# Second attention of a two-layer block: one run of scores and one run of outputs for each sequence, in place of two halves apart

## The chip, the core and the metric

The kernel runs on one core of one Trainium2 chip. The metric is the device time of one execution in microseconds (us); lower is better.

## The reference, cut to what matters

Sixteen sequences of 128 tokens of width 128 go through two blocks: cross attention and a mixture of experts, and then a second cross attention and a second mixture of experts. The change lies in the second attention. It has 16 heads of width 64 and reads the keys and values of a context of 128 tokens, the last 4 of which have weights of their own and a softmax of their own:

```python
def _attention(q_in, k_in, v_in):
    q = _split_heads(q_in); k = _split_heads(k_in); v = _split_heads(v_in)
    s = jnp.einsum('bhid,bhjd->bhij', q, k) * SCALE
    p = jax.nn.softmax(s, axis=-1)
    return _merge_heads(jnp.einsum('bhij,bhjd->bhid', p, v))
...
q_in = x @ Wq + _lora(x, q_down, q_up, q_alpha)
k_in = org_ctx @ Wk + _lora(org_ctx, k_down, k_up, k_alpha)
v_in = org_ctx @ Wv + _lora(org_ctx, v_down, v_up, v_alpha)
out = _attention(q_in, k_in, v_in)
out_ipa = _attention(q_in, ipa_ctx @ Wk_ipa, ipa_ctx @ Wv_ipa)
out = out + IPA_SCALE * out_ipa
return out @ Wo + bo + _lora(out, o_down, o_up, o_alpha)
```

## The kernel before

Each of the five engines runs a program of its own, in the order in which its code is written; nothing is scheduled by a planner. The engines meet only through semaphores: an instruction adds to one when it is done, and `wait_ge` holds an engine, with all that is queued behind it, until a count is there.

**The rounds.** Each engine walks through `body(b)` for b from -2 to 16. A round b works on three sequences: it takes the scores and the softmax of sequence b, prepares queries, keys and values of the next one, f = b + 1, and finishes the one before, t = b - 1 (the softmax weights are turned, multiplied by the values and projected). Rounds 1 to 14 have all three; round 0 has no t, and round 15 no f.

**The pieces on TensorE** (`@block.tensor`). `scores(b, half)` at line 1194 takes eight heads; a head is only 64 deep, so two heads lie on the upper and lower 64 rows of the array and follow each other as pairs. `turn(t, n)` (L1205, n from 0 to 3) transposes the weights of four heads. `queries(f, n)` (L1214), `keys(f, n)` (L1222) and `values(f, n)` (L1241) are projections in two halves each. `outputs(t, n)` (L1234) takes eight heads; a head's result is 64 wide, so two heads lie on the left and right 64 columns of the array. L1274 turns the normalized input of sequence b + 2, and L1282 is the output projection. Scores have the array cut in rows, outputs have it cut in columns, and all other pieces use it whole.

**PSUM.** Eight banks are shared out by hand. Scores use banks 0 to 3. Queries, turned weights and outputs go through banks 4 and 5, keys and turned weights through bank 6, values through banks 5 and 6, and the projection through bank 7. Each piece waits (`freed, count`) until the former content of its bank was copied out. Both halves of the keys go to bank 6, so `keys(f, 1)` waits on `Z.k0_sb` for the copy of the first half.

**VectorE** (`@block.vector`). `shifted(b, n)` (L664, L665, L667) takes the maxima of four heads and subtracts one from the four extra scores; ScalarE's exponentials wait for it. `turned(t, n)` (L673) copies turned weights out of PSUM. `summed(b, n)` (L679, L681) makes the sums and their reciprocals. L713 copies the first half of the keys to `k1T` and signals `Z.k0_sb`. L306, L310 and L301 are the residual, its statistics and the next normalized input.

**ScalarE** (`@block.scalar`). `powers(b, n)` (L923) takes four exponentials; `queries` (L930), `outputs` (L935) and `values` (L940) copy those results out of PSUM; L956 is the exponential of the extra scores, L961 the copy of the second half of the keys (`Z.k1_sb`), L967 the copy of the turned input.

**GpSimd** multiplies the weights by the reciprocals (L473), and SyncE loads the values of the four extra tokens by one DMA for each sequence. Neither is touched.

Of the kernel before, what the change touches and what calls it, by code (L numbers as in the profile page):

```python
# [26 lines left out]
CH = 4  # L27
# [15 lines left out]
def there(b):  # L43
    return not isinstance(b, int) or 0 <= b < B
# [19 lines left out]
def build_program(nc, T, out):  # L64

    with ExitStack() as ctx:
# [35 lines left out]
        class Arena:  # L102
# [9 lines left out]
            def take(self, shape, dt=F32):  # L112
# [8 lines left out]
                if dt != F32:  # L121
# [151 lines left out]
        Z = named(sem, "z", "xn xb tr xT q q_sb k0 k1 k0_sb k1_sb ki v v_sb vi0 vi1 score ipa_max maxed ipa_exp ipa_step ipa_p "  # L273
                            "exp sum rsum norm turned p_sb o o_sb proj x_new stats")
# [225 lines left out]
        def _(dve):  # L500
# [158 lines left out]
            def shifted(b, n):  # L659

                got_s = blocks(bank[n])
                part = slice(CH * n, CH * n + CH)
                dve.wait_ge(Z.score, CH * b + n + 1)
                dve.tensor_reduce(ipa_max[:, b % 2, part], got_s[:, :, ORG:S], X, ALU.max).then_inc(Z.ipa_max, 1)  # L664
                dve.tensor_reduce(negmax1[:, b % 2, part], got_s[:, :, 0:ORG], X, ALU.max, negate=True)  # L665
                dve.wait_ge(Z.ipa_max, CH * b + n + 1)
                dve.tensor_tensor(ipa_s[:, b % 2, part, :], got_s[:, :, ORG:S],  # L667
                                  ipa_max[:, b % 2, part].unsqueeze(2).broadcast_to((128, CH, IPA)), ALU.subtract).then_inc(Z.maxed, 1)
# [25 lines left out]
            def body(b):  # L694
                f, t = b + 1, b - 1
                if there(b):
                    shifted(b, 0)
                if there(t):
                    turned(t, 0)
                if there(b):  # L700
                    shifted(b, 1)
                if there(t):
                    turned(t, 1)
                if there(b):
                    summed(b, 0)
                    shifted(b, 2)
                if there(t):
                    turned(t, 2)
                if there(b):
                    shifted(b, 3)  # L710
                if there(f):
                    dve.wait_ge(Z.k0, f + 1)
                    dve.tensor_copy(k1T[:, f % 2, 0:4, 0:ORG], bank[6][:, 0:4 * ORG].rearrange("p (c n) -> p c n", c=4))\  # L713
                        .then_inc(Z.k0_sb, 1)
                if there(t):
                    turned(t, 3)
                if there(b):
                    summed(b, 1)
                    summed(b, 2)
                if there(b):  # L720
                    summed(b, 3)
                    ipa_norm(b)
                if there(t):
                    dve.wait_ge(Z.proj, t + 1)
                    dve.wait_ge(Z.xb, t + 1)
                    dve_residual(dve, Z, t, bank[7][:, 0:D])
                    dve_stats(dve, Z, t)
                if there(b + 3):
                    xn1_of(b + 3)
# [103 lines left out]
            with dve.Fori(0, B // 2) as i:  # L833
                for u in range(2):
                    b = i * 2 + u
# [4 lines left out]
        def _(act):  # L840
# [91 lines left out]
            def outputs(t, n):  # L932

                act.wait_ge(Z.o, 2 * t + n + 1)
                act.activation(o1T[:, 4 * n:4 * n + 4, :], blocks(bank[5 - n]), ACT.Copy).then_inc(Z.o_sb, 1)  # L935
# [6 lines left out]
            def body(b):  # L942
                f, t = b + 1, b - 1
                if there(b):
                    powers(b, 0)
                if there(f):
                    queries(f, 0)
                if there(b):
                    powers(b, 1)
                if there(f):  # L950
                    queries(f, 1)
                if there(b):
                    powers(b, 2)
                if there(b):
                    powers(b, 3)
                    act.activation(ipa_s[:, b % 2, :, :], ipa_s[:, b % 2, :, :], ACT.Exp).then_inc(Z.ipa_exp, 1)  # L956
                if there(t):
                    outputs(t, 0)
                if there(f):
                    act.wait_ge(Z.k1, f + 1)  # L960
                    act.activation(k1T[:, f % 2, 4:8, 0:ORG], bank[6][:, 0:4 * ORG].rearrange("p (c n) -> p c n", c=4), ACT.Copy)\  # L961
                        .then_inc(Z.k1_sb, 1)
                if there(t):
                    outputs(t, 1)
                if there(b + 2):
                    act.wait_ge(Z.tr, b + 3)
                    act.activation(xT[:, b % 2, :], bank[7][:, 0:128], ACT.Copy).then_inc(Z.xT, 1)  # L967
                if there(f):
                    values(f, 0)
                    values(f, 1)  # L970
# [53 lines left out]
        def _(pe):  # L1024
# [19 lines left out]
            def scores(b):  # L1044

                pe.wait_ge(A.negT_sb, b + 1)
                pe.wait_ge(A.qm, b + 1)
                pe.wait_ge(A.cT, 4)
                after(pe, A.exp, 2 * b)
                for g in range(CH):  # L1050
                    for i in range(4):
                        pe.matmul(SC0[:, i, 128 * g:128 * g + 128], pick0[tile_rows(i), g, :], negmax0T[tile_rows(i), b % 2, :],
                                  start=(g == 0), stop=False)
                for i in range(4):
                    mm = pe.matmul(SC0[:, i, :], k0T[tile_rows(i), b % 4, :], qm0[tile_rows(i), b % 4, :, :],  # L1055
                                   start=False, stop=True)
                    if i % 2 == 1:
                        mm.then_inc(A.score, 1)
# [166 lines left out]
            def outputs(t, n, freed, count):  # L1225

                pe.wait_ge(Z.p_sb, CH * t + 2 * n + 2)
                pe.wait_ge(Z.v_sb, 2 * t + n + 1)
                pe.wait_ge((Z.vi0, Z.vi1)[t % 2], 16 * (t // 2 + 1))
                after(pe, freed, count)  # L1230
                for c in range(CH):
                    for odd in range(2):
                        h = 8 * n + 2 * c + odd
                        mm = pe.matmul(blocks(bank[5 - n])[D1 * odd:D1 * odd + D1, c, :], v1[:, t % 2, D1 * h:D1 * h + D1],  # L1234
                                       p1T[:, CH * (2 * n + odd) + c, :], start=True, stop=True)
                mm.then_inc(Z.o, 1)
# [7 lines left out]
            def body(b):  # L1244
                f, t = b + 1, b - 1
                if there(b):
                    scores(b, 0)
                if there(t):
                    turn(t, 0, Z.o_sb, 2 * t)
                if there(f):  # L1250
                    queries(f, 0, Z.v_sb, 2 * f - 1)
                if there(t):
                    turn(t, 1, Z.v_sb, 2 * min(f, B))
                if there(f):
                    queries(f, 1, *((Z.p_sb, CH * t + 1) if there(t) else (Z.q_sb, 2 * f)))
                if there(b):
                    scores(b, 1)
                if there(t):
                    turn(t, 2, *((Z.q_sb, 2 * f + 1) if there(f) else (Z.v_sb, 2 * B - 1)))
                if there(f):  # L1260
                    keys(f, 0, *((Z.p_sb, CH * t + 2) if there(t) else (Z.v_sb, 2 * f)))
                if there(t):
                    turn(t, 3, *((Z.q_sb, 2 * f + 2) if there(f) else (Z.p_sb, CH * t + 1)))
                    outputs(t, 0, Z.p_sb, CH * t + 3)
                if there(f):
                    keys(f, 1, Z.k0_sb, f + 1)
                if there(t):
                    outputs(t, 1, Z.p_sb, CH * t + 4)
                if there(f):
                    values(f, 0, *((Z.o_sb, 2 * t + 1) if there(t) else (Z.q_sb, 2 * f + 1)))  # L1270
                if there(b + 2):
                    pe.wait_ge(Z.xn, b + 3)
                    after(pe, Z.x_new, b - 1)
                    pe.transpose(bank[7][:, 0:128], xn[:, b % 2, :], ident[:, :]).then_inc(Z.tr, 1)  # L1274
                if there(f):
                    values(f, 1, Z.k1_sb, f + 1)
                if there(t):
                    pe.wait_ge(Z.o_sb, 2 * t + 2)
                    after(pe, Z.xT, min(b + 3, B))
                    after(pe, Z.x_new, t)  # L1280
                    for c in range(8):
                        mm = pe.matmul(bank[7][:, 0:D], o1T[:, c, :], wo1[:, c, :], start=(c == 0), stop=(c == 7))  # L1282
                    mm.then_inc(Z.proj, 1)
# [101 lines left out]
```

## Time and profile before

| | |
|---|---|
| median of 3 runs | 611.37 us (610.2 to 611.38) |
| the profiled execution | 611.36 us, its span 609.7 us |
| TensorE busy | 517.7 us, 85% of the span |
| VectorE busy | 419.5 us, 69% |
| ScalarE busy | 288.1 us, 47% |
| GpSimd busy | 136.2 us, 22% |
| the second attention, first scores to last projection | 226.4 to 452.1 us |

The profile is of one execution. What a change within one stage is worth is read from that stage, by its timeline on each engine, not from the shares of the whole span. In the profile, a matmul in f32 has two records, so a group of eight matmuls is shown as x16. Starts of matmuls are recorded, while their ends are modelled and overlap the next group; a piece's cost is therefore read from its start to the start of the next piece.

### The profile page before, as it was taken

How to read it: one execution, taken by the hardware profiler on the slowest of the kernel's cores; microseconds unless marked ns; L12 is line 12 of the kernel's file. 1: busy time of each engine (PE TensorE's matmuls, PEld its weight loads, DVE VectorE, ACT ScalarE, POOL GpSimd, SP SyncE). 2: the span in 40 equal slices, each digit the busy share in tenths (PEclk: the TensorE clock that was granted, in tenths of full speed). 3: DMA queues.
4: the chain of work that ended last, by engine and by line, in shares of the span. 5: the costliest groups of instructions: out<-in, count | busy, mean ns of one | idle time of the engine just before them, and what ended most of it. 6: DMA issues, size and time to landing. Idle time of an engine off the chain costs nothing. (4 is left out here: it accounts for less than half of the span.)

```text
span 609.7 us, 13056 instructions
## 1 busy us (share of the span) xinstructions
PE 517.7 (85%) x4669; PEld 378.7 (62%) x4669; DVE 419.5 (69%) x1140; ACT 288.1 (47%) x728; POOL 136.2 (22%) x197
## 2 busy tenths in 40 slices
PE   1698888648999369999999999999856689999977
PEld 1455555437443157888888888888645335666667
DVE  3588888553769939777677777777653745777762
ACT  1354545212345227666555666666414473555530
POOL 3644433010000113333322233233420110000000
PEclk9989999975899979999999999999888799999989
DMA  7900000000000030000000000000000000222102
GB/s 177 212 3 3 2 2 3 2 1 1 0 1 1 1 110 1 4 2 3 2 3 4 2 3 2 3 3 3 2 0 1 1 0 27 79 77 77 53 4 66
DMA packets 21990, 14.35 MB, mean 24 GB/s; under 512 B 6056, under 2 KB 21264, under 8 KB 21936
## 3 DMA queue, kind: packets, MB, share of 16 engines
q1 hardware_dynamic: 21936, 13.61, 8.5%
q8 instruction: 36, 0.59, 0.4%
q14 instruction: 18, 0.15, 0.1%
HBM read 12.30 MB, written 1.05 MB: 22 GB/s over the span
## 5 line engine op out<-in xcount | busy, mean ns | idle before, releaser
L923 ACT ACTIVATE early<-bank,negmax 128x124 f32<-128x124 f32 x256 | 72.6, 375 | 62.0 <-DVE ipa_s L667 62.0
L473 POOL TENSOR_TENSOR early<-early,rsum 128x496 f32<-128x496 f32 x64 | 63.9, 1020 | 151.3 <-DVE rsum L681 151.3
L1342 PE MATMUL bank<-late,early 128*128 (+1 forms) x128 | 59.2, 608 | 2.0 <-ACTq L296 2.0
L863 ACT ACTIVATE early<-bank 128x1024 f32<-128x1024 f32 x32 | 31.0, 1022 | 30.6 <-PE bank L1055 30.6
L673 DVE COPY wide<-bank 128x512 f32<-128x512 f32 x64 | 43.2, 679 | 0.0
L665 DVE TENSOR_REDUCE negmax<-bank 128x4 f32<-128x496 f32 x64 | 42.4, 663 | 0.0
L548 DVE TENSOR_REDUCE negmax<-bank 128x8 bf16<-128x1024 f32 x32 | 39.0, 1220 | 4.2 <-PE bank L1040 3.8
L679 DVE TENSOR_REDUCE sums<-early 128x4 f32<-128x496 f32 x64 | 41.4, 647 | 0.5 <-ACT early L923 0.5
L815 DVE TENSOR_TENSOR late<-late,bank 128x512 f32<-128x512 f32 x32 | 22.0, 687 | 28.6 <-ACT late L1010 27.4
L1342 PEld LDWEIGHTS bank<-late,early 128*128 128x128 f32 x128 | 23.7, 195 | 27.4 <-issue 24.1
L1205 PE MATMUL bank<-ident,early 128*128 128x128 f32 x256 | 39.7, 280 | 1.1 <-DVE wide L673 1.1
L412 POOL TENSOR_TENSOR rstd<-veps,minus_half 128x14 f32<-128x14 f32 (+3 forms) x8 | 13.2, 1649 | 121.5 <-DVE veps L507 121.5
L306 DVE TENSOR_TENSOR x_all<-bank,x_all 128x128 f32<-128x128 f32 x32 | 9.2, 286 | 44.6 <-PE bank L1282 43.4
L1234 PE MATMUL bank<-wide,late 128*64 128x128 f32 x512 | 35.7, 283 | 2.7 <-DVE wide L673 2.7
L1282 PEld LDWEIGHTS bank<-late,wide 128*128 128x128 f32 x256 | 32.5, 200 | 8.8 <-issue 5.1
L1222 PE MATMUL bank<-cT_all,late 96*128 96x124 f32 x256 | 35.7, 283 | 1.9 <-DVE late L713 1.9
L1194 PE MATMUL bank<-late 64*128 64x128 f32 x512 | 37.2, 285 | 0.0
L1214 PE MATMUL bank<-xT,late 128*128 128x128 f32 x256 | 35.4, 285 | 0.4 <-ACT xT L967 0.4
L1354 PEld LDWEIGHTS bank<-early,late 128*128 128x128 f32 x256 | 30.9, 192 | 7.2 <-issue 7.2
L1178 PE MATMUL bank<-early 128*128 128x512 f32 x64 | 30.8, 609 | 4.9 <-DVE early L628 4.2
L1222 PEld LDWEIGHTS bank<-cT_all,late 96*128 96x128 f32 x256 | 31.4, 193 | 4.8 <-DVE late L713 4.7
L1194 PEld LDWEIGHTS bank<-late 64*128 64x128 f32 x512 | 31.1, 187 | 5.2 <-issue 1.7
(193 smaller groups left out, 1085.0 us busy)
## 6 DMA issues: line engine op xcount, KB each, us to landing
early<-in_L_ffn_w_dram SPq DMA_DIRECT2D x48, 128.0 KB, 2.2
out_dram<-x_all SPq DMA_DIRECT2D x16, 64.0 KB, 1.6
x_all<-in_x_dram SPq DMA_DIRECT2D x1, 768.0 KB, 6.9
ctx_all<-in_ctx_dram SPq DMA_DIRECT2D x1, 576.0 KB, 8.6
early<-in_L_ffn_We_dram SPq DMA_DIRECT2D x1, 512.0 KB
late<-in_L_xattn_Wq_dram SPq DMA_DIRECT2D x1, 512.0 KB, 6.8
late<-in_L_xattn_Wo_dram SPq DMA_DIRECT2D x1, 512.0 KB, 8.4
late<-in_L_xattn_Wk_dram SPq DMA_DIRECT2D x1, 384.0 KB, 6.6
```

The costliest lines, as they stand in the source:

```text
L473: pool.tensor_tensor(part, part, rsum1[:, b % 2, CH * n:CH * n + CH].unsqueeze(2).broadcast_to((128, CH, ORG)), ALU.mult).then_inc(Z.norm, 1)
L548: dve.tensor_reduce(to, MAX0.rearrange("p i (g n) -> p i g n", g=CH), X, ALU.max, negate=True)\
L665: dve.tensor_reduce(negmax1[:, b % 2, part], got_s[:, :, 0:ORG], X, ALU.max, negate=True)
L673: dve.tensor_copy(p1T[:, CH * n:CH * n + CH, :], blocks(bank[(4, 6, 5, 4)[n]])).then_inc(Z.p_sb, 1)
L679: dve.tensor_reduce(sums1[:, b % 2, part], p1[:, b % 2, n, :, 0:ORG], X, ALU.add).then_inc(Z.sum, 1)
L923: ins = act.activation(p1[:, b % 2, n, c, 0:ORG], blocks(bank[n])[:, c, 0:ORG], ACT.Exp, bias=negmax1[:, b % 2, CH * n + c:CH * n + c + 1])
L1194: mm = pe.matmul(blocks(bank[2 * half + odd])[:, c, :], q1T[rows, b % 2, CH * half + c, :], k1T[rows, b % 2, CH * half + c, :], start=True ...
L1205: mm = pe.transpose(blocks(bank[(4, 6, 5, 4)[n]])[:, c, :], p1[:, t % 2, n, c, :], ident[:, :])
L1214: mm = pe.matmul(blocks(bank[5 - n])[:, c, :], wq1[:, part], xT[:, f % 2, :], start=True, stop=True)
L1222: mm = pe.matmul(bank[6][:, ORG * c:ORG * c + ORG], wk1[0:C, part], cT_all[:, f, 0:ORG], start=True, stop=True)
L1234: mm = pe.matmul(blocks(bank[5 - n])[D1 * odd:D1 * odd + D1, c, :], v1[:, t % 2, D1 * h:D1 * h + D1], p1T[:, CH * (2 * n + odd) + c, :], s ...
L1342: mm = pe.matmul(bank[2 * c + n][:, :], w[:, q % 4, 128 * c:128 * c + 128], xgT[:, :, e, :], start=True, stop=True)
```

## The change

The same instructions with the same operands run on each engine; only their order is another. On TensorE, `scores(b, 1)` follows `scores(b, 0)` at once, and `outputs(t, 0)` stands behind `keys(f, 1)`, right before `outputs(t, 1)`. On VectorE, the copy of the first half of the keys stands ahead of `shifted(b, 3)`. On ScalarE, `outputs(t, 0)` stands behind the copy of the second half of the keys.

```diff
@@ VectorE, body(b)
                 if there(t):
                     turned(t, 2)
-                if there(b):
-                    shifted(b, 3)
                 if there(f):
                     dve.wait_ge(Z.k0, f + 1)
                     dve.tensor_copy(k1T[:, f % 2, 0:4, 0:ORG], bank[6][:, 0:4 * ORG].rearrange("p (c n) -> p c n", c=4))\
                         .then_inc(Z.k0_sb, 1)
+                if there(b):
+                    shifted(b, 3)
                 if there(t):
                     turned(t, 3)
@@ ScalarE, body(b)
-                if there(t):
-                    outputs(t, 0)
                 if there(f):
                     act.wait_ge(Z.k1, f + 1)
                     act.activation(k1T[:, f % 2, 4:8, 0:ORG], bank[6][:, 0:4 * ORG].rearrange("p (c n) -> p c n", c=4), ACT.Copy)\
                         .then_inc(Z.k1_sb, 1)
                 if there(t):
+                    outputs(t, 0)
                     outputs(t, 1)
@@ TensorE, body(b)
                 if there(b):
                     scores(b, 0)
+                    scores(b, 1)
                 if there(t):
                     turn(t, 0, Z.o_sb, 2 * t)
...
                 if there(f):
                     queries(f, 1, *((Z.p_sb, CH * t + 1) if there(t) else (Z.q_sb, 2 * f)))
-                if there(b):
-                    scores(b, 1)
                 if there(t):
                     turn(t, 2, *((Z.q_sb, 2 * f + 1) if there(f) else (Z.v_sb, 2 * B - 1)))
                 if there(f):
                     keys(f, 0, *((Z.p_sb, CH * t + 2) if there(t) else (Z.v_sb, 2 * f)))
                 if there(t):
                     turn(t, 3, *((Z.q_sb, 2 * f + 2) if there(f) else (Z.p_sb, CH * t + 1)))
-                    outputs(t, 0, Z.p_sb, CH * t + 3)
                 if there(f):
                     keys(f, 1, Z.k0_sb, f + 1)
                 if there(t):
+                    outputs(t, 0, Z.p_sb, CH * t + 3)
                     outputs(t, 1, Z.p_sb, CH * t + 4)
```

TensorE in round 1, before, from the first scores (L1194) over turn (L1205), queries (L1214), keys (L1222) and outputs (L1234) to the second outputs:

```order
L1194 MATMUL bank<-late 128x128 x8
L1205 MATMUL bank<-ident,early 128x128 x4
L1214 MATMUL bank<-xT,late 128x128 x4
L1205 MATMUL bank<-ident,early 128x128 x4
L1214 MATMUL bank<-xT,late 128x128 x4
L1194 MATMUL bank<-late 128x128 x8
L1205 MATMUL bank<-ident,early 128x128 x4
L1222 MATMUL bank<-cT_all,late 128x124 x4
L1205 MATMUL bank<-ident,early 128x128 x4
L1234 MATMUL bank<-wide,late 64x128 x8
L1222 MATMUL bank<-cT_all,late 128x124 x4
L1234 MATMUL bank<-wide,late 64x128 x8
```

The same stretch of the changed kernel, where the line numbers of these pieces are lower by one:

```order
L1193 MATMUL bank<-late 128x128 x16
L1204 MATMUL bank<-ident,early 128x128 x4
L1213 MATMUL bank<-xT,late 128x128 x4
L1204 MATMUL bank<-ident,early 128x128 x4
L1213 MATMUL bank<-xT,late 128x128 x4
L1204 MATMUL bank<-ident,early 128x128 x4
L1221 MATMUL bank<-cT_all,late 128x124 x4
L1204 MATMUL bank<-ident,early 128x128 x4
L1221 MATMUL bank<-cT_all,late 128x124 x4
L1233 MATMUL bank<-wide,late 64x128 x16
```

Four pieces on a cut array have become two of twice the length, and between the two halves of the keys there is now one turn, in place of a turn and an outputs piece.

VectorE in round 1, before, from `shifted(b, 2)` on: L664, L665 and L667 are one `shifted`, L673 is a `turned`, L713 the copy of the first half of the keys:

```order
L664 TENSOR_REDUCE ipa_max<-bank 128x4
L665 TENSOR_REDUCE negmax<-bank 128x4
L667 TENSOR_TENSOR ipa_s<-bank,ipa_max 128x16
L673 COPY wide<-bank 128x512
L664 TENSOR_REDUCE ipa_max<-bank 128x4
L665 TENSOR_REDUCE negmax<-bank 128x4
L667 TENSOR_TENSOR ipa_s<-bank,ipa_max 128x16
L713 COPY late<-bank 128x4x124
L673 COPY wide<-bank 128x512
```

The same stretch of the changed kernel, where that copy is line 711:

```order
L664 TENSOR_REDUCE ipa_max<-bank 128x4
L665 TENSOR_REDUCE negmax<-bank 128x4
L667 TENSOR_TENSOR ipa_s<-bank,ipa_max 128x16
L673 COPY wide<-bank 128x512
L711 COPY late<-bank 128x4x124
L664 TENSOR_REDUCE ipa_max<-bank 128x4
L665 TENSOR_REDUCE negmax<-bank 128x4
L667 TENSOR_TENSOR ipa_s<-bank,ipa_max 128x16
L673 COPY wide<-bank 128x512
```

The copy has moved ahead of one `shifted`, three instructions.

## Rows read from the trace of the kernel before

**Rows 1.** Windows (stretch, length, busy time of engines, PEclk): rounds; end of stage.

```profile
222.00:437.00 215.00, 211.11 (x2013) 177.17 (x2012) 162.12 (x478) 133.06 (x392) 68.78 (x89) 1.00 0.02 6
437.00:443.90 6.90, 6.02 (x35) 5.65 (x36) 3.08 (x11) 1.84 (x6) 4.69 (x7) 0.51 0.01 2
```

**Rows 2.** Timeline of TensorE, round 6: start us, us, instruction, [idle before <- releaser].

```profile
305.07 1.16 PE L1194 MATMUL bank<-late 64*128 64x128 f32 x16
306.16 0.66 PE L1205 MATMUL bank<-ident,early 128*128 128x128 f32 x4
306.65 1.06 PE L1214 MATMUL bank<-xT,late 128*128 128x128 f32 x8
307.55 0.60 PE L1205 MATMUL bank<-ident,early 128*128 128x128 f32 x4
307.98 1.06 PE L1214 MATMUL bank<-xT,late 128*128 128x128 f32 x8
308.97 1.16 PE L1194 MATMUL bank<-late 64*128 64x128 f32 x16
310.06 0.66 PE L1205 MATMUL bank<-ident,early 128*128 128x128 f32 x4
...
311.45 0.60 PE L1205 MATMUL bank<-ident,early 128*128 128x128 f32 x4
311.98 1.09 PE L1234 MATMUL bank<-wide,late 128*64 128x128 f32 x16
313.00 1.16 PE L1222 MATMUL bank<-cT_all,late 96*128 96x124 f32 x8
314.09 1.09 PE L1234 MATMUL bank<-wide,late 128*64 128x128 f32 x16
315.11 1.12 PE L1241 MATMUL bank<-late,cT_all 96*124 96x512 f32 x2
...
318.92 1.16 PE L1194 MATMUL bank<-late 64*128 64x128 f32 x16
```

**Rows 3.** Timeline of TensorE at the first and last rounds.

```profile
232.88 1.16 PE L1222 MATMUL bank<-cT_all,late 96*128 96x124 f32 x8 [1.16 <-DVE late L713]
...
437.19 1.97 PE L1234 MATMUL bank<-wide,late 128*64 128x128 f32 x16 [0.25 <-DVE wide L673]
...
447.37 1.97 PE L1234 MATMUL bank<-wide,late 128*64 128x128 f32 x32 [0.57 <-DVE wide L673]
```

**Rows 4.** Timeline of VectorE, round 6.

```profile
306.26 0.17 DVE L664 TENSOR_REDUCE ipa_max<-bank 128x4 f32<-128x16 f32 x1 [0.22 <-PE bank L1194]
...
307.01 0.68 DVE L673 COPY wide<-bank 128x512 f32<-128x512 f32 x1
307.61 0.16 DVE L664 TENSOR_REDUCE ipa_max<-bank 128x4 f32<-128x16 f32 x1
...
312.26 0.66 DVE L713 COPY late<-bank 128x496 f32<-128x496 f32 x1
312.84 0.68 DVE L673 COPY wide<-bank 128x512 f32<-128x512 f32 x1
313.44 0.66 DVE L679 TENSOR_REDUCE sums<-early 128x4 f32<-128x496 f32 x1
...
314.22 0.64 DVE L679 TENSOR_REDUCE sums<-early 128x4 f32<-128x496 f32 x1
```

**Rows 5.** Timeline of ScalarE, round 6.

```profile
307.13 1.13 ACT L923 ACTIVATE early<-bank,negmax 128x124 f32<-128x124 f32 x4 [3.14 <-DVE ipa_s L667]
308.13 0.61 ACT L930 ACTIVATE late<-bank 128x512 f32<-128x512 f32 x1
308.61 1.16 ACT L923 ACTIVATE early<-bank,negmax 128x124 f32<-128x124 f32 x4
...
313.38 0.27 ACT L956 ACTIVATE ipa_s<-ipa_s 128x64 f32<-128x64 f32 x1
313.52 0.61 ACT L935 ACTIVATE wide<-bank 128x512 f32<-128x512 f32 x1
```

## The prediction

> **What bounds the kernel now.** I first read the windows of the profile over the second attention. From 222 to 437 us TensorE is busy 211.1 of 215.0 us, at a granted clock of 1.00, while VectorE has 162.1 us and ScalarE 133.1 us [rows 1]. So I next read TensorE's timeline for one round. From the scores at 305.07 to those at 318.92 us no row has an idle time: the round lasts 13.85 us and is pure TensorE time [rows 2]. Rounds 1 to 14 repeat it (scores start at 235.80 us in round 1 and every 13.85 us after). A shorter TensorE order therefore shortens the kernel, but only until another engine is late. For that I then read the timelines of VectorE and ScalarE for the same round [rows 4, 5]. All times below with no other zero are counted from the round's first scores, so 305.07 is 0.
>
> **TensorE: what is saved.** The reader should compare how long the same piece takes by its neighbours [rows 2].
> - Queries take 0.90 (306.65 to 307.55) before a turn, but 0.99 (307.98 to 308.97) before scores.
> - A turn takes 0.43 between whole-array pieces (307.55 to 307.98), 0.49 behind scores (306.16 to 306.65), and 0.53 before outputs (311.45 to 311.98).
> - Scores take 1.09. Turn 2 and the first keys together take 1.39 (310.06 to 311.45), so these keys take 0.90, as queries do.
> - Outputs take 1.02 each, and the second keys, between two of them, take 1.09.
>
> Each border between a cut and a whole array thus costs about 0.1 on the piece outside, and some more lies inside the cut piece. In the last round two outputs pieces follow each other: 1.97 for x32, against 1.09 for x16 alone [rows 3, 2], so a second outputs piece adds 0.88 and not 1.02. For scores no row shows two pieces in a row. The bounds are 1.09 (nothing saved inside) and 0.90 (eight pairs at the pace of the eight records of queries); I take 0.90, since outputs behave so.
>
> The new round on TensorE, if nothing waits: scores 1.09 + 0.90 = 1.99; turn 0.49; queries 0.90; turn 0.43; queries 0.90; turn 0.43; keys 0.90; turn 0.43; keys before outputs 0.99; outputs 1.02 + 0.88 = 1.90; and from the first values to the next scores 3.81, unchanged (315.11 to 318.92). The sum is 13.17, which is 0.68 less than 13.85. Over 14 rounds that would be 9.5 us.
>
> **The cover that goes.** The second keys need bank 6, and so wait for VectorE's copy of the first keys. Before, this copy ran from 312.26 to 312.92, and the keys began at 313.00 [rows 4, 2]: it landed just in time, 0.08 ahead. The change takes 1.0 us of outputs away from before these keys, and 1.1 us of scores too. In return it moves the copy ahead of one `shifted`. I walk VectorE's chain up to the copy.
> - The first `shifted` starts at 1.19, as before; it waits for the first half of the scores only [rows 4]. It takes 0.75 (306.26 to 307.01), to 1.94.
> - Then comes the first `turned`. Before, its turn was long done. Now the turn starts at 1.99, behind all scores, and ends at 2.65 (0.66 after its start [rows 2]). With the 0.03 that VectorE takes to follow (scores end at 305.07 + 1.16 = 306.23, and it starts at 306.26) this `turned` starts at 2.68: a **new wait of 0.74** at the head of the chain.
> - From there it runs through: `turned` 0.60 (307.01 to 307.61), `shifted` 0.75, `turned` 0.60, `summed` 0.78 (313.44 to 314.22), `shifted` 0.75, `turned` 0.60. That is 4.08, so the copy starts at 6.76 and ends at 7.42. What these steps wait for is earlier: the second turn starts at 3.38 and ends at 3.98, before 4.03; the scores of banks 2 and 3 are ready at 2.0.
> - The second keys start 0.08 later, at 7.50.
>
> TensorE reaches them at 1.99 + 0.49 + 0.90 + 0.43 + 0.90 + 0.43 + 0.90 + 0.43 = 6.47. So it stands **idle for 1.03 us** there in each round. Bounds: were all of VectorE's steps as short as their issue allows and turn 0 followed at once, the copy could come 0.1 earlier; if the two scores pieces take 2.18 instead of 1.99, turn 0 and all of the chain come 0.19 later. Queued behind the waiting keys is all of TensorE's round: both outputs, values, projection and the next scores.
>
> **After the stall.** Keys 0.99, to 8.49; outputs 1.90, to 10.39, where the first values start if bank 5 is free. For that ScalarE must have copied the first outputs. The fourth `shifted` now starts behind the copy, at 6.76 + 0.58 (312.26 to 312.84) = 7.34. Exponentials start 0.87 after their `shifted` (306.26 to 307.13), at 8.21, and take 1.00 (307.13 to 308.13); the extra exponential 0.14 (313.38 to 313.52), to 9.35; the copy of the second keys 0.48 (as 308.13 to 308.61), to 9.83; the copy of the outputs ends 0.61 later, at 10.44 [rows 5]. TensorE follows some 0.05 behind, since the 0.08 above is an upper end: the values start at 10.49, another 0.10 late. Then 3.81: the round ends at **14.30**. Bounds for this second wait are 0 and 0.13.
>
> So a round goes from 13.85 to 14.30, up 0.45: 0.68 saved, 1.03 + 0.10 lost. The second outputs need the fourth `turned`, which ends at 7.34 + 0.75 + 0.68 = 8.77, before 9.4. VectorE's remaining sums end near 11.8 and its residual waits for the projection as before. GpSimd's multiplications follow these sums, and what needs them is the second to fourth turn of the next round, from 14.30 + 3.38 on. These cost nothing, with more than a microsecond of cover. SyncE's small DMA of the extra values waits for the second outputs of a round and is needed a round later. It has some ten microseconds of cover.
>
> **The edges.** Round 0 has no turn. There the second keys already wait 1.16 us for the copy [rows 3], and the copy moves ahead by one `shifted`, 0.75, and by the wait for later scores; but ScalarE's own copy of the second keys, behind all exponentials, is next late. I take -0.2, between 0 and -1.0. In round 15 there are no keys; all outputs wait for VectorE's chain (the second at 437.19 has such a wait [rows 3]), which gets the new 0.74 of turn 0 and loses nothing: +0.7.
>
> **Sum.** 14 x 0.45 = 6.3, - 0.2 + 0.7 = +6.8. The span of the profiled run, 609.7 us, becomes 616.5, and with the 1.66 outside it (611.36 - 609.7), 618.2. The median of the runs, 611.37, is the same as this execution. With the cheap ends of the bounds (stall 0.9, no second wait, round 0 at -1.0) a round is 14.07 and the time 614; with the dear ends for the waits 14.35 and 619.
>
> **Two rules beside the rows.** The Trainium skill, on the page TensorEngine Tiling (Array Packing), section Key Properties, says that a change of tiling mode drains TensorE. By that rule alone the result is the 9.5 us gain above, since four such borders go in each round; rows 2 bear it out in size. The same page, section PSUM Bottleneck, says that a faster TensorE can leave the copies out of PSUM as the limit. By it the result is 14.30 a round; VectorE's copy at 312.26 with 0.08 to spare is where the trace agrees.
>
> **Rivals.**
> - *The cover holds, and the saving arrives* (faster). This needs the copy to start by about 5.8 instead of 6.76, that is, the wait at turn 0 must not be there or VectorE must catch it up. For it: VectorE is only 75% busy in the stage [rows 1]. Against: its free time lies behind its sums, while the chain from first scores to the copy has no slack left. A round of 13.17 gives -9.5 - 0.2 + 0.7: 602.4 us. Chance 0.08.
> - *Saving and stall cancel.* With a stall of only 0.6 to 0.75 the round is within 0.1 of 13.85, and the time within 1.2 us (0.2%, about what a measurement here can tell) of 611.4. Nothing in the rows makes the chain 0.4 shorter. Chance 0.06.
> - *Borders don't cost what I think* (the change doesn't do what it says): each group of eight carries its own cost. Then scores take 2.18 and outputs 2.04, turn 0 and so the keys come 0.19 later, and the round is 7.69 + 0.99 + 2.04 + 3.81 = 14.53: 14 x 0.68 + 0.9 gives 621.8. The x32 row of 1.97 speaks against [rows 3]. Chance 0.06.
> - *The clock falls.* With over 1 us idle in a round the granted clock could fall as it did at 437 us, where outputs took 1.97 for x16 instead of 1.09 and the stretch 437.0 to 443.9 has 0.51 [rows 3, 1]. A stretch like that costs about half of its 6.0 us of TensorE time, 3 us. Against: a wait of 1.16 us in round 0 left it at 1.00 [rows 3, 1]. Two such stretches give 624. Chance 0.06.
>
> **How the numbers follow.** The forecast has 0.70 (618.2), and 0.04 is left for dearer things I don't see. Slower: 0.70 + 0.06 + 0.06 + 0.04 = 0.86; same 0.06; faster 0.08. The range takes in the forecast with its bounds and the two dear rivals: 613.5 to 624. It leaves out the faster case, the cancelling one and the dearest.
>
> **What would show it.** Right: TensorE's timeline has 1.0 us idle before the second keys in each round, released by VectorE's copy; VectorE has 0.7 idle before its first `turned`, released by the turn; the scores' x32 takes about 2.0 and the outputs' 1.9; the first values have about 0.1 idle, released by ScalarE; rounds are 14.2 to 14.4 apart. Wrong: no idle before the second keys, or a first `turned` that starts at 1.9; scores that take 2.2; or a clock below 1.00 between rounds 1 and 14.

## The result and the profile after

| | before | changed |
|---|---|---|
| median | 611.37 us (6 runs, 605.15 to 611.75) | 617.14 us (6 runs, 614.01 to 618.85) |
| the profiled execution | 611.36 us, span 609.7 | 618.85 us, span 617.2 |
| TensorE busy | 517.7 us | 513.8 us |
| a round of the second attention (1 to 14) | 13.85 us | 14.27 us |

The ratio is 1.0107, 95% interval 1.0061 to 1.0154: the kernel became slower by 1.1%, although TensorE is busy 3.9 us less. (The medians alone lie 5.8 us apart, 0.9%.)

TensorE's timeline of round 5 of the changed kernel answers to [rows 2]. Its lines are lower by one, the projection's by two: 1193 are scores, 1204 turns, 1213 queries, 1221 keys, 1233 outputs, 1240 values, 1280 the projection.

```profile
294.06 2.06 PE L1193 MATMUL bank<-late 64*128 64x128 f32 x32
296.05 0.66 PE L1204 MATMUL bank<-ident,early 128*128 128x128 f32 x4
296.54 1.06 PE L1213 MATMUL bank<-xT,late 128*128 128x128 f32 x8
297.44 0.60 PE L1204 MATMUL bank<-ident,early 128*128 128x128 f32 x4
297.87 1.06 PE L1213 MATMUL bank<-xT,late 128*128 128x128 f32 x8
298.77 0.60 PE L1204 MATMUL bank<-ident,early 128*128 128x128 f32 x4
299.20 1.05 PE L1221 MATMUL bank<-cT_all,late 96*128 96x124 f32 x8
300.09 0.60 PE L1204 MATMUL bank<-ident,early 128*128 128x128 f32 x4
301.51 1.16 PE L1221 MATMUL bank<-cT_all,late 96*128 96x124 f32 x8 [0.82 <-DVE late L711]
302.60 1.97 PE L1233 MATMUL bank<-wide,late 128*64 128x128 f32 x32
304.52 1.12 PE L1240 MATMUL bank<-late,cT_all 96*124 96x512 f32 x2
...
308.33 2.06 PE L1193 MATMUL bank<-late 64*128 64x128 f32 x32
```

From scores to scores it is 14.27 us. The scores of 16 heads take 1.99 (294.06 to 296.05), and the outputs 1.92. Up to the last turn TensorE is ahead by what the scores' borders gave. Then comes the only idle time of the round: the second keys start 1.42 behind the turn (300.09 to 301.51), where a turn takes 0.43. That is 0.99 us lost; the row shows 0.82, since the modelled end of the turn overlaps it.

VectorE, same round, answers to [rows 4]. L711 is the copy of the first keys:

```profile
295.25 0.17 DVE L664 TENSOR_REDUCE ipa_max<-bank 128x4 f32<-128x16 f32 x1 [0.22 <-PE bank L1193]
...
296.74 0.69 DVE L673 COPY wide<-bank 128x512 f32<-128x512 f32 x1 [0.65 <-PE bank L1204]
...
298.69 0.66 DVE L679 TENSOR_REDUCE sums<-early 128x4 f32<-128x496 f32 x1
...
300.80 0.66 DVE L711 COPY late<-bank 128x496 f32<-128x496 f32 x1
301.38 0.16 DVE L664 TENSOR_REDUCE ipa_max<-bank 128x4 f32<-128x16 f32 x1
```

The first `turned` (L673) starts 2.68 after the scores, released by the turn on TensorE. Without that wait it would have started at 1.94, as in [rows 4]. From there nothing waits until the copy, which starts at 6.74 and ends at 7.40; the keys follow at 7.45.

ScalarE, same round: L935 are the copies of both outputs. The first of the two ends near 304.46 (0.61 after its start, as such a copy takes in [rows 5]), the first values start at 304.52:

```profile
303.38 0.60 ACT L959 ACTIVATE late<-bank 128x496 f32<-128x496 f32 x1
303.85 1.37 ACT L935 ACTIVATE wide<-bank 128x512 f32<-128x512 f32 x2
```

The list of waits from 227 to 440 us, rounds 0 to 14 and the first turns of round 15, shows how often. Its columns are total us, times, longest:

```profile
PE bank L1221 <- DVE late L711: 12.2, 15, 0.8
DVE wide L673 <- PE bank L1204: 9.8, 15, 0.7
PEld bank L1240 <- ACT wide L935: 2.7, 14, 0.2
```

### The profile page after: what moved, and what is told of

Its sections match the earlier page's. It is cut to its first block and busy times, and to the rows that moved or that the text cites. A ratio compares the mean times of both kernels' runs of the same rounds, so it can differ in the third digit from the quotient of the medians.

```text
span 617.2 us, 13056 instructions
## 1 busy us (share of the span) xinstructions
PE 513.8 (83%) x4669; PEld 377.7 (61%) x4669; DVE 419.5 (68%) x1140; ACT 288.9 (47%) x728; POOL 136.1 (22%) x197
## 5 line engine op out<-in xcount | busy, mean ns | idle before, releaser
L673 DVE COPY wide<-bank 128x512 f32<-128x512 f32 x64 | 43.4, 681 | 9.8 <-PE bank L1204 9.8
L665 DVE TENSOR_REDUCE negmax<-bank 128x4 f32<-128x496 f32 x64 | 42.4, 663 | 0.0
L548 DVE TENSOR_REDUCE negmax<-bank 128x8 bf16<-128x1024 f32 x32 | 39.1, 1221 | 3.3 <-PE bank L1039 2.9
L1177 PE MATMUL bank<-early 128*128 128x512 f32 x64 | 32.6, 639 | 4.9 <-DVE early L628 4.2
L1233 PE MATMUL bank<-wide,late 128*64 128x128 f32 x512 | 32.6, 280 | 3.6 <-DVE wide L673 3.6
L1280 PE MATMUL bank<-late,wide 128*128 128x128 f32 x256 | 33.1, 285 | 1.4 <-ACT wide L935 1.4
L1240 PE MATMUL bank<-late,cT_all 96*124 96x512 f32 x64 | 33.4, 616 | 0.4 <-ACT late L959 0.4
```

Source lines behind the costliest of these rows:

```text
L548: dve.tensor_reduce(to, MAX0.rearrange("p i (g n) -> p i g n", g=CH), X, ALU.max, negate=True)\
L673: dve.tensor_copy(p1T[:, CH * n:CH * n + CH, :], blocks(bank[(4, 6, 5, 4)[n]])).then_inc(Z.p_sb, 1)
```

## The experiments

Each ratio below is to the kernel before, run beside the experiment (its median was 610.49 us beside the first four and 611.47 beside the last three). The length of a round is the better measure, since only the order within it was changed.

Two kinds of theory were to be told apart. Mine: each switch between a cut and a whole array costs TensorE some 0.17 us (the forecast's 0.68 over four), the change saves four of them a round, and it loses more because the copy of the first keys no longer lands in time. The rivals: the run of scores itself, or VectorE's whole chain, sets the pace whatever stands behind; or the saving is not in the switches.

### Scores together, outputs apart

The changed kernel, with the outputs and ScalarE's copies back in the old order (the cut shows TensorE only). VectorE's order stays as changed.

```diff
                 if there(t):
                     turn(t, 3, ...)
+                    outputs(t, 0, Z.p_sb, CH * t + 3)
                 if there(f):
                     keys(f, 1, Z.k0_sb, f + 1)
                 if there(t):
-                    outputs(t, 0, Z.p_sb, CH * t + 3)
                     outputs(t, 1, Z.p_sb, CH * t + 4)
```

> Only the scores follow one another; the outputs stand apart as before, and VectorE's copy of the first keys stays ahead of the fourth shifted, as in the changed kernel. My theory (the second keys wait for VectorE's copy because 1.0 us of outputs no longer stands before them): the copy still ends 7.4 us into the round, but the second keys now come 1.0 us later, so their wait goes. Instead the first outputs wait some 0.3 us for the third turned (bank 5). Round 13.8 us (13.85 before, 14.27 in the changed kernel), time 611.5. Rival (the run of scores itself is what costs, since VectorE's chain starts 0.7 us later and sets the round, whatever TensorE's order behind it is): round 14.2 or more, time 617.

Measured: 611.06 us, ratio 1.0017 (0.996 to 1.0074), so no difference. Rounds are 13.91 us. TensorE, in this kernel L1232 outputs, L1220 keys:

```profile
299.41 0.60 PE L1203 MATMUL bank<-ident,early 128*128 128x128 f32 x4
300.35 1.09 PE L1232 MATMUL bank<-wide,late 128*64 128x128 f32 x16 [0.33 <-DVE wide L673]
301.37 1.16 PE L1220 MATMUL bank<-cT_all,late 96*128 96x124 f32 x8
```

The wait is no longer before the keys but before the outputs in front of them, for the third `turned`, and it is 0.41 by starts (0.94 behind the turn, against 0.53 in [rows 2]). It eats what the borders of the scores gave. Those are 0.34 by [rows 2]: 0.19 in the second scores, 0.09 on the queries before them and 0.06 on the turn behind. So 13.85 - 0.34 + 0.41 = 13.92. The rival's 14.2 did not come, though VectorE had the same late start.

### Outputs together, scores apart

The changed kernel, with the second scores back where they stood before.

```diff
                 if there(b):
                     scores(b, 0)
-                    scores(b, 1)
...
                     queries(f, 1, ...)
+                if there(b):
+                    scores(b, 1)
```

> Only the outputs follow one another, with the copies on VectorE and ScalarE moved as in the changed kernel; the scores stand apart as before. My theory: VectorE has no wait at its first turned, but the second half of the scores now stands before turn 2, so the copy ends at 7.2 us, and the second keys would start at 6.8: they wait 0.5 us. Round 14.1 us, time 615.2. Rival (the run of scores is what costs): this change alone saves its borders, round 13.5 us, time 607.

Measured: 614.12 us, ratio 1.0081 (1.0028 to 1.0135); rounds 14.13 us. L1219 are the keys:

```profile
298.62 0.60 PE L1202 MATMUL bank<-ident,early 128*128 128x128 f32 x4
299.55 1.16 PE L1219 MATMUL bank<-cT_all,late 96*128 96x124 f32 x8 [0.33 <-DVE late L711]
300.63 1.97 PE L1231 MATMUL bank<-wide,late 128*64 128x128 f32 x32
```

Here VectorE does not start late, and the keys still wait, 0.50 by starts (0.93 against 0.43). So the loss does not need the run of scores: taking the outputs from between the two halves of the keys is enough for a loss of 0.28 us a round.

### The copy put back behind the fourth shifted

The changed kernel, with one VectorE piece moved.

```diff
                     turned(t, 2)
+                if there(b):
+                    shifted(b, 3)
                 if there(f):
                     dve.wait_ge(Z.k0, f + 1)
                     ...
-                if there(b):
-                    shifted(b, 3)
```

> The changed kernel with VectorE's copy of the first keys put back behind the fourth shifted. My theory: the copy is on the path that sets the round, so 0.75 us more before it shows: second keys 1.7 us idle by the natural order, round 14.9 to 15.0 us (14.27 in the changed kernel), time 626. Rival (VectorE's whole round or ScalarE sets the pace, not this copy): the order of two VectorE pieces doesn't matter, round 14.3, time 617.

Measured: 640.88 us, ratio 1.0507 (1.0438 to 1.0576). The direction is as my theory had it, but the size is double: some 30 us above the kernel before, where 626 would have been 15. Four of the 14 rounds take 14.99 us, as expected; ten take 16.62. TensorE in one of the long ones (L1219 keys, L1231 outputs), and two windows: the first over most of these outputs, the second over what follows, up to the next scores. After stretch, length and the busy time of the five rows of engines, their last columns are the granted clock, the DMA share and GB/s:

```profile
309.56 1.16 PE L1219 MATMUL bank<-cT_all,late 96*128 96x124 f32 x8 [1.57 <-DVE late L713]
310.65 3.01 PE L1231 MATMUL bank<-wide,late 128*64 128x128 f32 x32
313.58 1.71 PE L1238 MATMUL bank<-late,cT_all 96*124 96x512 f32 x2
```

```profile
311.40:314.80 3.40, 3.40 (x26) 2.55 (x21) 1.54 (x7) 1.19 (x2) 3.11 (x5) 0.50 0.00 0
314.80:318.00 3.20, 3.20 (x23) 2.29 (x21) 0.00 (x0) 1.36 (x3) 0.00 (x0) 1.00 0.03 5
```

The wait is 1.57 us instead of 0.82 in all 14 rounds. In ten of them the granted clock then falls from 1.00 to 0.50, that is from 2.4 to 1.2 GHz: the outputs take 2.93 by starts instead of 1.89, the values 1.55 instead of 0.96, and together 1.63 us more are lost. So the copy is on the path that sets the round, and with a wait that is 0.75 us longer the clock fell too, though not in every round: the four short ones have the same wait. In the changed kernel itself the clock stayed at 1.00 from round 1 to round 14.

### VectorE takes a shifted where it had to wait for the turn

The changed kernel, with VectorE's first pieces in another order.

```diff
                     shifted(b, 0)
+                    shifted(b, 1)
                 if there(t):
                     turned(t, 0)
                 if there(b):
-                    shifted(b, 1)
+                    summed(b, 0)
                 if there(t):
                     turned(t, 1)
                 if there(b):
-                    summed(b, 0)
                     shifted(b, 2)
```

> The changed kernel with VectorE's order shifted 0, shifted 1, turned 0, summed 0, turned 1: what it does at 1.94 us is then a shifted, whose scores are there, and not a turned that must wait for turn 0. My theory: the 0.74 us of new wait at the first turned is the cause of half of the stall; without it the copy ends 0.5 us earlier (it then waits 0.2 us for the keys themselves), the second keys wait 0.5 instead of 1.0 us, round 13.76 us, time 610. Rival (the order before the copy doesn't matter, or the wait at the turn only moves slack): round 14.27, time 617.

Measured: 609.29 us, ratio 0.9991 (0.9946 to 1.0037): no slower than before, with rounds of 13.78 us. L1219 are the keys:

```profile
295.44 1.05 PE L1219 MATMUL bank<-cT_all,late 96*128 96x124 f32 x8
296.33 0.60 PE L1202 MATMUL bank<-ident,early 128*128 128x128 f32 x4
297.25 1.16 PE L1219 MATMUL bank<-cT_all,late 96*128 96x124 f32 x8 [0.33 <-DVE late L711]
298.34 1.97 PE L1231 MATMUL bank<-wide,late 128*64 128x128 f32 x32
```

The wait at the turn was 0.5 of the 0.99 us, and its removal gives just that back (14.27 to 13.78). The rest is the missing cover, and no order on VectorE can win it. The list of waits from 250 to 430 us has the copy itself waiting for the first keys, in ten of its rounds:

```profile
DVE late L711 <- PE bank L1219: 1.5, 10, 0.2
```

VectorE is early now, and the copy can't start before its keys are done. From the start of the first keys to that of the second it is 1.81 us (295.44 to 297.25). With one turn between the two, TensorE has only 0.89 + 0.43 = 1.32 us of work for it, and 0.49 stay idle. The kernel before had 2.44 us between the two starts, from this row to 313.00 in [rows 2]:

```profile
310.56 1.05 PE L1222 MATMUL bank<-cT_all,late 96*128 96x124 f32 x8
```

### Both outputs ahead of the second keys

The change with cover put back. TensorE does both outputs before the second keys; ScalarE copies in the new order. VectorE's round begins with shifted 0, shifted 1, turned 0, turned 1, shifted 2, turned 2, shifted 3, turned 3; then come the copy of the first keys and all four summed.

```diff
@@ TensorE
                     turn(t, 3, ...)
-                if there(f):
-                    keys(f, 1, Z.k0_sb, f + 1)
-                if there(t):
                     outputs(t, 0, Z.p_sb, CH * t + 3)
                     outputs(t, 1, Z.p_sb, CH * t + 4)
                 if there(f):
+                    keys(f, 1, Z.k0_sb, f + 1)
                     values(f, 0, ...)
@@ ScalarE
+                if there(t):
+                    outputs(t, 0)
+                    outputs(t, 1)
                 if there(f):
                     act.wait_ge(Z.k1, f + 1)
                     ...
-                if there(t):
-                    outputs(t, 0)
-                    outputs(t, 1)
```

> The changed kernel with the second keys behind both outputs (TensorE: turn 3, outputs 0, outputs 1, keys 1; ScalarE copies in that order), VectorE in the order shifted 0, shifted 1, turned 0, turned 1, shifted 2, turned 2, shifted 3, turned 3, copy of the first keys, and then the four summed. Both runs stay together, and the 1.9 us of outputs cover the copy. My theory (the change failed only by the cover it took away): no wait on TensorE, the copy ends near 7.4 us and the second keys start at 8.4 us; round 13.17 us, time 601 to 602. Rival (whatever the order, VectorE or ScalarE can't deliver a round in much less than 13.8 us once the scores come in one run): round 13.7 or more, time 609 or more.

Measured: 600.21 us, ratio 0.9825 (0.9799 to 0.9851). It beats both kernels. The round is 13.26 us, without idle time on TensorE (L1189 scores, L1200 turns, L1229 outputs, L1217 keys, L1236 values):

```profile
300.38 2.06 PE L1189 MATMUL bank<-late 64*128 64x128 f32 x32
...
306.41 0.60 PE L1200 MATMUL bank<-ident,early 128*128 128x128 f32 x4
306.94 2.06 PE L1229 MATMUL bank<-wide,late 128*64 128x128 f32 x32
308.94 1.16 PE L1217 MATMUL bank<-cT_all,late 96*128 96x124 f32 x8
309.93 1.02 PE L1236 MATMUL bank<-late,cT_all 96*124 96x512 f32 x2
...
313.64 2.06 PE L1189 MATMUL bank<-late 64*128 64x128 f32 x32
```

VectorE's copy starts at 307.68 and would end at 308.35, 0.59 ahead of the keys. So the runs of scores and of outputs do pay, 0.59 us a round, once nothing waits. (TensorE's, VectorE's and ScalarE's order changed together here; which of the three it needs was not tried.) The rival, that VectorE or ScalarE can't deliver a round much below 13.8, falls. I had expected 13.17. The sum was 0.09 short, since I had used the changed kernel's: here the turn has outputs behind it and takes 0.53 instead of 0.43, the outputs take 2.00 (306.94 to 308.94) instead of 1.90, and from the first values to the next scores it is 3.71 instead of 3.81. The two runs do not pay alike. From the first scores to the first keys' end it is 6.03 instead of 6.38, so the scores' run gives 0.35. From there to the next scores it is 7.23 instead of 7.47, so the outputs' run gives 0.24.

### A turn between the two scores

```diff
                 if there(b):
                     scores(b, 0)
-                    scores(b, 1)
                 if there(t):
                     turn(t, 0, Z.o_sb, 2 * t)
+                if there(b):
+                    scores(b, 1)
                 if there(f):
                     queries(f, 0, Z.v_sb, 2 * f - 1)
```

(against the kernel of the last experiment)

> As keys_last, but turn 0 stands between the two scores pieces (scores 0, turn 0, scores 1, queries 0). The work is the same and nothing new waits, so the round shows what one more pair of borders between a cut and a whole array costs. My theory: 0.34 us more (0.10 on the turn's or queries' side, the rest inside the second scores): round 13.51 us, 14 to 16 x 0.34 = 5 us more than keys_last. Rival (what is saved lies in the halves' own start, or in banks, not in the switch): scores behind a turn cost no more than scores behind scores, round 13.2 us.

Measured: 606.81 us, ratio 0.9927 (0.9891 to 0.9962); rounds 13.65 us, 0.39 more, and again no idle time:

```profile
303.96 1.16 PE L1189 MATMUL bank<-late 64*128 64x128 f32 x16
305.06 0.66 PE L1200 MATMUL bank<-ident,early 128*128 128x128 f32 x4
305.64 1.16 PE L1189 MATMUL bank<-late 64*128 64x128 f32 x16
306.73 1.16 PE L1209 MATMUL bank<-xT,late 128*128 128x128 f32 x8
307.73 0.60 PE L1200 MATMUL bank<-ident,early 128*128 128x128 f32 x4
```

The two scores pieces take 1.10 + 1.09 instead of 1.99, the turn between them 0.58 instead of 0.49, and the queries behind scores 1.00 instead of 0.89. One more pair of borders is 0.39 us, where I had expected 0.34. It is the neighbour that costs, not the piece: the rival of a cost in the halves' own start falls.

### The changed kernel once more

> The changed kernel again, beside keys_last on the same chip. Theory: rounds of 14.27 us with 0.8 us idle shown before the second keys, time 617, some 15 us above keys_last. Rival: a few us of the difference to the kernel before come from stages ahead of the second attention; then its time moves with the start of the first scores, and the rounds stay at 14.27.

Measured: 616.94 us, ratio 1.0098 (1.0063 to 1.0133), rounds 14.28 us, first scores at 225.29 us where the first profile of it had 227.73. So the rounds repeat to 0.01 us, while the start of the stage moves by 2.4 us between executions of one kernel. In the stretch from 126 to 157 us TensorE's granted clock was 0.52 in the first profile and 0.67 in this one. The spans differ by less, 617.2 and 615.7 us, so what follows the rounds moves too. That such stages make the spread of the single times is likely, but only these two profiles show it. It is why the rounds tell more than the totals.

## Why the prediction was right, point by point

Forecast 618.2, measured 617.14, and slower with 0.86. The mechanism came as forecast; inside the sum two terms were off, and the total hides it.

**What TensorE saves: somewhat less.** Scores 1.99 as forecast, outputs 1.92 for 1.90. The value taken for two scores in a row, 0.90 added and not 1.09, had no row of before behind it; it came out as the outputs' pace had suggested. But the second keys take 1.09 (301.51 to 302.60) and not 0.99, which I had taken from pieces that follow a turn; behind a wait they are as long as [rows 2] showed them between two outputs. Without the idle time the round is 14.27 - 0.99 = 13.28, so 0.57 is saved and not 0.68: 0.35 by the scores, as the 0.34 of the rows, and 0.22 by the outputs. That each of the four borders gives 0.17 holds for the scores only.

**The cover that goes: right, to 0.05 us.** The first `turned` starts at 2.68 (forecast 2.68), the copy at 6.74 (6.76), the keys at 7.45 (7.50), lost 0.99 (1.03). The walk through VectorE's chain with durations of before was enough, since no duration changed.

**After the stall: the wait for ScalarE is there, but hardly shows.** The forecast had keys of 0.99, TensorE ready for the values at 10.39, and ScalarE's copy of the first outputs releasing them at 10.49. Measured, the longer keys bring TensorE there at about 10.43 (7.45 + 1.09 + 1.89, the outputs' length in a short round with the copy put back, 327.27 to 329.16). ScalarE's copy ends near 10.40 for the 10.44 forecast, and the values start at 10.46. The later of the two decides, so the keys' error cost nothing, and of the second wait of 0.10 some 0.03 is left. That this error of 0.10 fell where a wait had already been counted is luck. The 0.2 us on the weight load [the third line of the waits] is no measure of ScalarE's delay: with the copy put back, the same load has 0.17 idle where ScalarE had itself been waiting for the outputs. The round is 14.27 for 14.30: 0.57 saved and 0.99 lost, for the 0.68 and 1.13 of the forecast.

**The edges: right.** Round 0 went from 9.40 to 9.26 (-0.14, forecast -0.2): the keys' wait fell from 1.16 to 0.77, and the second values then waited 0.39 for ScalarE's copy of the second keys, which the prediction had named as next late. In round 15, from the scores to the second outputs, 7.56 became 8.30 (+0.74, forecast +0.7).

**The sum.** Rounds 1 to 14 give 199.66 - 193.83 = +5.83 us (forecast 6.3, whose 0.45 a round should have been 0.42). With the edges it is +6.43 of the 6.8. The profiled executions differ by 7.5 in span, of which 1.33 us lie before the first scores (226.40 and 227.73), in stages whose code is the same. The ratio of the runs, 1.0107, is 6.5 us, the medians differ by 5.8. A single total is thus right to a few us at best, and the hit to 1.1 us is in part luck; the 0.42 a round is what the prediction rests on.

**The rivals.** That the cover holds was false here, and true in the kernel with both outputs first. That borders cost nothing is refuted by the turn between two scores. That saving and stall cancel was not the change's case, but is that of its half with only the scores together, and of the reordered VectorE. That the clock falls did not happen at 0.99 us lost a round, and did with the copy put back, at 1.74, in ten rounds of 14.

**The two rules.** The Trainium skill, TensorEngine Tiling (Array Packing), section Key Properties, says that a change of tiling mode drains TensorE. No trace here shows a drain as such; they show a price, 0.39 us for one more pair of borders at the scores and 0.22 to 0.24 for the pair that the outputs' run saves. The section PSUM Bottleneck says that copies out of PSUM may become the bottleneck. In the changed kernel the copy of the first keys does set the round. But it was a matter of order, and not of how much is copied: with the same copies in another order the round is 13.26 and TensorE the limit again, busy 196.9 of 198.0 us (222 to 420).

## What to carry to other kernels

Grouping pieces of one array shape saves TensorE the switches, but each piece that is moved was also a cover for some copy between its neighbours. Look for pieces that share a PSUM bank, find how early the copy between them lands, and keep at least that much TensorE work there. Here the piece, its copy and the hand-over took 1.81 us at best, from the first use of the bank to the second. And when a long run delays the first result that an in-order engine takes next, give that engine something whose input is already there.

## What was not expected of the hardware

A wait of TensorE that grew from 0.82 to 1.57 us as shown, by one move on VectorE, went with a fall of the granted clock from 1.00 to 0.50 for part of the round in 10 of 14 rounds. It cost 1.63 us in each of these: more than twice what the longer wait cost by itself (14.27 to 14.99). Where between the two waits this sets in was not tried, nor why four rounds with the same wait kept the clock.

The cost of a border shows on both of its sides: 0.09 to 0.11 on each whole-array piece beside a cut one (turn 0.58 for 0.49, queries 1.00 for 0.89), and 0.20 in the cut pieces (2.19 for 1.99). The keys, whose rows show 96 rows of the array in use and not 128, have no such cost beside a turn: 0.89, as the queries.
